# Row 0's experts as timed tasks among the scans of layer 0, and seven PSUM banks as one stock in layer 1

## What is computed

```python
def _L0_ffn_ref(x, scores, expert_weights, top_experts, w1, w2):   # w1 (256, 2048), w2 (2048, 256)
    order = jnp.argsort(flat_experts, stable=True)
    token_idx = order // TOP_K
    h = jax.nn.gelu(x_flat[token_idx] @ w1, approximate=True)
    y = h @ w2
    out = jnp.zeros((T, H)).at[token_idx].add(w_sorted[:, None] * y)
...
def _mamba_block(x, ...):
    xm, res = jnp.split(x @ in_proj_w.T, 2, axis=-1)
    xm = silu(conv(xm) + conv_b)                       # causal, 4 taps, per channel
    dt, Bm, Cm = jnp.split(xm @ x_proj_w.T, ...)
    delta = softplus(dt @ dt_proj_w.T + dt_proj_b)
    # h[t] = exp(delta[t] A) h[t-1] + delta[t] B[t] u[t];  y[t] = sum over 16 states of C[t] h[t]
    y = (scan(...) + u * D) * silu(res)
    return y @ out_proj_w.T
...
x = x + _L0_attn_ref(layernorm(x), ...) + _L0_ffn_ref(layernorm(x), ...)
x = x + _L1_attn_ref(layernorm(x), ...) + _L1_ffn_ref(layernorm(x), ...)
```

## Time and profile before

| | |
|---|---|
| median of 3 runs | 4269.71 us (4264.41 to 4275.40) |
| the profiled execution | 4272.54 us, span 4270.8 us |
| busy: PE, DVE, ACT, POOL | 3918.5, 3170.8, 2571.6, 2199.5 us |
| granted TensorE clock, mean | 0.955 of full speed |
| first scan; last gate of layer 0 | 187.73 us; 2022.57 us |

### The profile page before, as it was taken

The page is one execution under the profiler, slowest core; times in us unless marked ns, Lnnn a source line. Parts: engine busy times, 40 slices in busy tenths (PEclk is TensorE's granted clock), DMA queues, the critical chain, the costliest instruction groups (busy, mean ns, idle before and its releaser), DMA issues.

```text
span 4270.8 us, 60828 instructions
## 1 busy us (share of the span) xinstructions
PE 3918.5 (92%) x19232; PEld 2262.9 (53%) x19232; DVE 3170.8 (74%) x6060; ACT 2571.6 (60%) x3951; POOL 2199.5 (51%) x1724
## 2 busy tenths in 40 slices
PE   7988899999999899997889999999999999999997
PEld 4555555656565555565545545455455444544444
DVE  0299999999999999989474856748567585765753
ACT  3387778787888778775244454545554545545444
POOL 0299999999999899998211313213131131321311
PEclk9989999999999999998989999999999989999898
DMA  2254445545555555544311221212212122121210
GB/s 107 71 163 153 162 154 161 163 161 163 165 164 166 150 164 164 166 144 158 107 41 53 75 62 39 76 53 74 63 46 69 53 73 64 39 76 53 63 41 19
DMA packets 250177, 442.02 MB, mean 103 GB/s; under 512 B 25780, under 2 KB 80388, under 8 KB 248964
## 3 DMA queue, kind: packets, MB, share of 16 engines
q1 hardware_dynamic: 249860, 438.14, 33.1%
HBM read 366.39 MB, written 69.21 MB: 102 GB/s over the span
## 4 chain that ended last, share of the span: by engine, by line
PE 48%; DVE 8%; issue 4%; ACT 4%; POOL 2%; DMA 1%; SPq 0%; DVEq 0%; POOLq 0%; ACTq 0%
PE ps L1345 7%; PE ps L1453 6%; PE ps L1446 5%; PE ps L1307 5%; PE ps L1326 5%; PE ps L1376 3%; PE ps L1382 2%; DVE ps L1843 2%; PE ps L1209 2%; PE ps L1353 1%; PE ps L1429 1%; PE ps L1387 1%; DVE ps L1821 1%; PE ps L1258 1%; PE ps L1416 1%
## 5 line engine op out<-in xcount | busy, mean ns | idle before, releaser
L2066 POOL TENSOR_TENSOR drive<-du,b_wide 128x1024 f32<-128x1024 f32 x512 | 1201.1, 2361 | 173.1 <-DVE held L1821 96.9
L1470 ACT ACTIVATE exps<-ps 128x1024 f32<-128x1024 f32 (+3 forms) x768 | 620.4, 809 | 591.8 <-PE ps L1326 565.9
L2101 POOL TENSOR_SCALAR_AFFINE_SELECT exps<-exps 128x256 f32<-128x256 f32 x512 | 213.2, 419 | 1374.8 <-ACT exps L1470 1373.1
L1470 ACT ACTIVATE ps<-delta,neg_a 128x512 f32<-128x512 f32 x1024 | 681.0, 685 | 147.3 <-DVE heavy L1799 127.3
L1843 DVE CUSTOM_DVE_ANT_0 ps<-ps,later 128x128 f32<-128x128 f32 (+3 forms) x1024 | 484.4, 512 | 208.9 <-PE ps L1307 202.2
L1258 PE MATMUL ps<-p_all,heavy 128*128 128x128 f32 x3072 | 452.2, 283 | 89.4 <-DVE heavy L1799 78.7
L1258 PEld LDWEIGHTS ps<-p_all,heavy 128*128 128x128 f32 x3072 | 368.9, 145 | 257.3 <-DVE heavy L1799 139.8
L1799 DVE TENSOR_TENSOR heavy<-c_wide,ps 128x512 f32<-128x512 f32 x704 | 468.5, 670 | 1.0
L1821 DVE TENSOR_TENSOR_SCAN ps<-ps,carry,drive 128x512 f32<-128x512 f32 x352 | 441.2, 1272 | 16.7 <-ACT ps L1470 16.7
L1821 DVE TENSOR_TENSOR_SCAN ps<-ps,drive 128x512 f32<-128x512 f32 x352 | 420.6, 1214 | 26.2 <-ACT ps L1470 22.9
L1846 DVE TENSOR_REDUCE smax<-ps 128x2 f32<-128x1024 f32 x256 | 312.6, 1221 | 136.1 <-PE ps L1307 131.2
(11 more groups left out here) (193 smaller groups left out, 6475.3 us busy)
## 6 DMA issues: line engine op xcount, KB each, us to landing
b_wide<-bc_dram SPq DMA_DIRECT2D x512, 256.0 KB, 3.4
c_wide<-bc_dram SPq DMA_DIRECT2D x512, 256.0 KB, 3.6
stacks<-parts SPq DMA_DIRECT2D x192, 256.0 KB, 2.4
qs<-stacks SPq DMA_DIRECT2D x128, 192.0 KB
ks<-stacks SPq DMA_DIRECT2D x128, 192.0 KB, 4.2
x_row<-in_x SPq DMA_DIRECT2D x15, 1024.0 KB, 8.0
resid<-mix SPq DMA_DIRECT2D x9, 1024.0 KB, 5.3
x_row<-resid SPq DMA_DIRECT2D x9, 1024.0 KB, 6.5
```

What stands on the lines that cost most here:

```text
L1470: return nc.scalar.activation(out_, in_, func, **kw)
L2066: G.tensor_tensor(drive[:, g % DRIVE_SLOTS, :, :], du[:, e, :, :], wide(b_wide[:, g % B_SLOTS, :], MD), ALU.mult).then_inc(driven, 1)
```

## The change

Experts: `moe_pre0`, the loop above, `mlp_down`, `moe1`, `moe2` and `moe_h` are gone. The expert MLP is now four passes v (two halves of the hidden channels r, two halves of the row c), each of 8 `mh` units (up, copied by ACT into `h0`), one `gelu_t` of ACT over all of `h0`, and 4 `mo` units (down), which DVE adds to `mix` one by one. They are tasks of layer 0's list with ticks 32 steps a pass from tick 0 on, in the banks 6 and 7. Their weights go, a quarter of the experts' total at a time, through `w_up0` and `w_down0`, the buffers of the MLP of layer 0: SP loads the second halves (`expert_up`, `expert_down`), then the MLP's own weights (`up`, `down`), and stores row 0 (`first`) as tasks of the list. `h` of j = 0 comes after the last `mo`. The prelude keeps `xt` of the first half, `xm`, `cv`, `xd` and `dl` of j = 0; `res` of j = 0, the second half's `norm` and `xt` join the list. The row statistics of row 0 are taken in two halves, and x and the weights are loaded in two parts each.

Banks in layer 1: the pair [0, 1] becomes a third place for wide units, and a dense unit may take any of seven banks: bank 3 if it is free, else one whose neighbour is taken, else any.

```diff
 LENGTH0 = {..., "o": 4.0, "mu": 0.4, "var": 0.4, "mh": 1.74, "mo": 3.5}
+MOE_FROM, MOE_STEPS = 0, 32
...
+def moe_part(v):
+    return v // NC, v % NC
...
 def prelude_units():
-    out = [("xt", 0, c, k) for c in range(NC) for k in range(KD)]
-    for i in range(NC * ME):
-        out += moe_pre0(i) + [("moe", i // ME, i % ME)]
-    return out
+    return ([("xt", 0, 0, k) for k in range(KD)] + [("xm", 0, m) for m in range(MI)] + [("cv", 0, m) for m in range(MI)]
+            + [("xd", 0)] + [("dl", 0, m) for m in range(MI)])
...
+    for t in range(TC, NT):
+        add("a", ("norm", 0, t), 0.42 if t > TC else 3.2, t - TC - 2)
+    for c, k in [(1, k) for k in range(KD)]:
+        add("p", ("xt", 0, c, k), LENGTH0["xt"], 2 + k, ("a", "norm", 0, NT - 1))
+        add("a", ("xt", 0, c, k), EMPTY0["xt"], 2 + k, ("p", "xt", 0, c, k))
+    for t in range(TC):
+        add("p", ("res", 0, t), LENGTH0["res"], 26 + 2 * t)
+        add("a", ("res", 0, t), EMPTY0["res"], 26 + 2 * t, ("p", "res", 0, t))
+    add("a", ("silu_g", 0), 4.5, 36, ("a", "res", 0, TC - 1))
+    for v in range(MOE_PASSES):
+        r, c = moe_part(v)
+        at = MOE_FROM + MOE_STEPS * v
+        for m in range(MF):
+            add("p", ("mh", v, m), LENGTH0["mh"], at + MOE_STEPS * m / 16, ("a", "xt", 0, c, KD - 1),
+                ("p", "mo", v - 1, TC - 1) if v else None, only(r and c == 0, ("s", "expert_up")))
+            add("a", ("mh", v, m), EMPTY0["mh"], at + MOE_STEPS * m / 16, ("p", "mh", v, m))
+        add("a", ("gelu_t", v), 6.2, at + MOE_STEPS / 2, ("a", "mh", v, MF - 1))
+        for t in range(TC):
+            place = at + MOE_STEPS / 2 + MOE_STEPS * t / 8
+            add("p", ("mo", v, t), LENGTH0["mo"], place, ("a", "gelu_t", v), only(r and c == 0, ("s", "expert_down")))
+            add("v", ("mo", v, t), EMPTY0["mo"], place, ("p", "mo", v, t))
...
-WIDE_BANKS = ([4, 5], [6, 7])
-DENSE_BANKS = ([0], [1], [3])
+WIDE_BANKS = ([4, 5], [6, 7], [0, 1])
+DENSE_BANKS = ([3], [0], [1], [4], [5], [6], [7])
+PARTNER = {0: 1, 1: 0, 4: 5, 5: 4, 6: 7, 7: 6}
...
         if name in needs:
-            held[unit] = min(pools[pool_of(unit)], key=lambda pool: pool[0])
-            held[unit][0] = float("inf")
-            banks[unit] = held[unit][1]
+            fit = [choice for choice in choices[pool_of(unit)] if from_when(choice) <= start]
+            banks[unit] = min(fit, key=lambda one: (len(one[1]) == 1 and one[1][0] in PARTNER and
+                                                    1 + (bank_free[PARTNER[one[1][0]]] <= start), from_when(one)))[1]
+            for bank in banks[unit]:
+                bank_free[bank] = float("inf")
...
-            sp.dma_start(x_row0[:, :, :], x_in[0].rearrange("(t p) d -> p t d", p=P)).then_inc(x_fetched, 16)
-            sp.dma_start(moe1[:, :, :], moe1_in).then_inc(moe_in, 16)
-            sp.dma_start(w_l0[:, :], w_in[:, 0:L0_COLS]).then_inc(weights_in, 16)
-            sp.dma_start(moe2[:, :, :], moe2_in).then_inc(moe_in, 16)
+            for half, signal in ((slice(0, TC), x_first), (slice(TC, NT), x_fetched)):
+                sp.dma_start(x_row0[:, half, :], x_in[0].rearrange("(t p) d -> p t d", p=P)[:, half, :]).then_inc(signal, 16)
+                if half.start == 0:
+                    sp.dma_start(w_l0[:, 0:W_AT["in"][1]], w_in[:, 0:W_AT["in"][1]]).then_inc(weights_in, 16)
+            sp.dma_start(w_l0[:, W_AT["in"][1]:], w_in[:, W_AT["in"][1]:L0_COLS]).then_inc(weights_more_in, 16)
+            load_experts(0, True)
+            load_experts(0, False)
             sp.dma_start(mix[:, :, :], x_in[0].rearrange("(t p) d -> p t d", p=P)).then_inc(x0_in, 16)
...
+                elif kind == "expert_up":
+                    full(sp, L0_PLAN, ("mh", NC - 1, MF - 1))
+                    load_experts(1, True)
...
+                elif kind == "mh":
+                    r, c = moe_part(j)
+                    m = unit[2]
+                    drained(pe, L0_PLAN, ("xt", 0, c, KD - 1), "a")
+                    pe.wait_ge(expert_up_in, 16 * (r + 1))
+                    for k in range(KD):
+                        last = mm(bank, w_up0[:, k, m * P:(m + 1) * P], xT0[:, k, c * HALF:(c + 1) * HALF],
+                                  start=(k == 0), stop=(k == KD - 1))
+                elif kind == "mo":
+                    t = unit[2]
+                    pe.wait_ge(expert_gelu, j + 1)
+                    pe.wait_ge(expert_down_in, 16 * (moe_part(j)[0] + 1))
+                    for m in range(MF):
+                        last = mm(bank[:, 0:D], h0[:, m, t * P:(t + 1) * P], w_down0[:, m, :], start=(m == 0),
+                                  stop=(m == MF - 1))
...
+                elif kind == "gelu_t":
+                    drained(act, L0_PLAN, ("mh", j, MF - 1), "a")
+                    f(h0[:, :, :], h0[:, :, :], ACT.Gelu_apprx_tanh).then_inc(expert_gelu, 1)
...
+                elif kind == "mo":
+                    (r, c), tt = moe_part(task[1]), task[2]
+                    t = TC * c + tt
+                    bank = full(dve, L0_PLAN, task)
+                    V.scalar_tensor_tensor(mix[:, t, :], bank[:, 0:D], ew_sum[:, t:t + 1], mix[:, t, :], ALU.mult,
+                                           ALU.add).then_inc(drained_v, 1)
```

235 lines of the change are left out of this document (112 added, 123 removed).

## The result

The changed kernel takes 4168.23 us (median of 4 runs, 4166.9 to 4176.46) against 4272.56 us for the kernel before on the same chip (4 runs, 4264.41 to 4283.51). The ratio is 0.9758, with a 95% interval of 0.9732 to 0.9784: faster by 2.4%. The profiled execution has a span of 4173.8 us where the one of before had 4270.8, that is 97.0 us less. The forecast was 4180. By the medians the gain is 104.3 us: the profiled execution of the changed kernel happens to be the slowest of its four.

What follows compares the result with a forecast made beforehand. PE was busy 92% of the span; in the scans DVE set about 55 us per pair, PE where its share was large. Terms -121 + 60 + 5 - 38 = -94 from 4272.5 gave 4178.5, stated as 4180 us, range 4115 to 4245.

Steps and rivals of the forecast that it cites:

- the signs: Profile if right: first scan 65 to 72, pair 3's gate 283 us later, last gate near 1967, layer 1 some 2209 us.
- signs of being wrong: Drive waits for b_wide after experts' loads; PE waits for gelu; layer 1 single-unit bank waits or clock below 0.95.
- Term 1: Start: with the experts moved out, the first scan comes at 67 instead of 187.7 us: -121 us (-116 to -123).
- Term 2: Scans: expert work lengthens pairs 0 to 3 by 55 us, pairs 4 to 7 by 1, ACT's gelu 4: +60 (+45 to +85).
- PE sets it: Scan pairs: where PE's share is large, PE sets the time; pairs 0 to 3 take 275 x 1.03 = 283 us.
- here PE is late anyway, so I put 1 us each: Pairs 0 to 3: DVE idles if decays run dry during ACT's four gelu passes, priced at +4 us.
- Term 3: SP's queue: four 1 MB loads and row 0's store among b_wide and c_wide loads: +5 us (0 to +30).
- Term 4: Layer 1: seven banks as one stock remove 40% of 92 us of waits, times 1.1: -38 us (-95 to +30).
- (a): Layer 1: the banks give nothing, 4214 us, or lose 30 on single banks, 4245 us; chance 0.19.
- (b): Both parts at their better end, term 2 at 45 and term 4 at -85: some 4110 us; chance 0.13.
- (c): Scans: PE stays at 91%, the first scan's lead is spent, banks alone decide: 4232 to 4270 us; chance 0.04.
- (d): Layer 1: some 740 single units each wait 0.25 us longer for their bank: slower, 4307 us; chance 0.05.

Runs made afterwards that it cites:

- e5: Changed kernel with the loops of each expert unit (mh, mo) cut to their first matmul call, same instruction order: 4163.49 us, ratio 0.974.
- e12: Changed kernel with expert units cut to their first matmul call and the list planned anew for the shorter units: 4163.47 us, ratio 0.9734.
- e7: On top of e3, row 0's second half normalised early, two transposed blocks and two mh units moved between cv and xd: 4135.66 us, ratio 0.9679.
- e3: Changed kernel with PARTNER emptied, so single units take whichever of seven banks has been free longest: 4144.85 us, ratio 0.9679.
- e8: Changed kernel with an expert pass every 48 scan steps instead of 32, spread over pairs 0 to 5: 4193.78 us, ratio 0.982.
- e10: Changed kernel with expert units cut to their first matmul call and each gelu pass replaced by a one-column copy: 4154.15 us, ratio 0.97.
- e1: Changed kernel with layer 1's old banks, so the experts' part alone: 4219.86 us, ratio 0.986.
- e4: Changed kernel with single units limited to banks 3, 0 and 1, scores keeping three pairs: 4181.29 us, ratio 0.9765.
- e6: Changed kernel with the second loads of the experts' weights cut from 1 MB to 4 KB each: 4167.89 us, ratio 0.9752.
- e2: Kernel before with only the planner's stock of seven banks, experts still ahead of the scans: 4224.3 us, ratio 0.9868.

## Why the prediction was right, and where a step was not

**Sum.** -94 forecast, -97.0 in the two profiles; four terms within 7 us each. One of them doesn't come out of its own working: 40% of 92 us, times 1.1, is 40.5 and not 38. Of the signs, first scan, gate of pair 3, PE's share and clock are as written; layer 1 took 2202.2 us for 2209; the last gate ended at 1971.6 for "near 1967", in four other executions with the same layer 0 at 1961.1 to 1966.3. Of the signs of being wrong, PE waited once for ACT's copy of an experts' tile (4.2 us), and layer 1's clock is 0.94, as in the kernel before over the whole layer.

**Term 1, the start: right in size and in its steps.** -120.1 instead of -121. One place was off: xd took 6.24 us where 3.44 and "perhaps a slow clock again" stood; its copy was out at 52.6, not 50, and dl, softplus, du and the first drive product followed some 2.6 us late. The margin between 65 and 67 took up 2 of these. The landing of b_wide did not matter. A table load again began right behind the copy before it (41.66 + 0.69 = 42.35, load at 42.37) and silu right behind the load (43.66), so the extra drain that the Trainium skill's page "ScalarE: Activation LUTs", section "What ACT_TABLE_LOAD costs", gives per switch does not show here either.

**Term 2, the experts in the scans: right in size, wrong in cause.** +60 forecast, +60.8 measured; pairs 0 to 3 in 284.8 us for 283, at PE 95% and clock 0.98, as written. The failed step is "PE sets it", PE work times 1.03. Taking 76 us of PE's work out gave 8.4 us of the 56.2 that the stretch had grown by (e5); with a newly planned list it gave 18.1, of which part came back later (e12); and moving two mh units and two transposes into an idle place gave nothing in these pairs (e7 against e3). The row that I should have weighed is the one I wrote off with "here PE is late anyway, so I put 1 us each": DVE waits 35 us for decays, 28 more than before, and its own work in these pairs is 10.3 us more (228.1 against 217.8). In the new list ACT copies 32 h tiles out, runs four gelu passes and 25 table loads (20 in those pairs of before), and the decays stand in one queue with all of it: 31.6 of the 35 us end behind a load back to the exponential, as the trace shows above. That several engines, each in a fixed order, hold the stretch in turn, so that no single removal gives back its own time, is my reading of this. That PE's 95% and the count times 1.03 gave the number was luck; e8 breaks it: the same PE work in 529.3 us.

What stays open: with PE's expert work and the gelu passes both gone (e10), pairs 0 to 3 still take 268.0 us, 39.4 more than before. DVE's busy time accounts for 9.3 of it (227.2 - 217.8), its waits for decays for 17.4 (24.4 in e10 against 7.0), and smaller waits of several kinds for the rest. Where the late decays stand is in the trace; that ACT's fixed order, with the switches of function and the copies between them, makes the waits was not tried, neither by moving the passes nor by a list planned anew without both.

The +7.3 from pair 8 on, for which I had no term, is that one execution's and not the change's: in the same stretch e1, e3, e4 and e6 take 1387.8, 1385.8, 1385.6 and 1387.7 us with the same order as the changed kernel, and the kernel before 1386.1.

**Term 3, SP's loads: 5 forecast, nothing found,** inside its bounds. Two of the four transfers cost nothing (e6). The queue's own waits stay in that run, but drive products wait for b_wide only twice in pairs 0 to 7, for 3.1 us at 87.6, before any of the loads, and for 1.9 us at 354.5, behind the store and the last load; in the kernel before it is 3.4 + 1.1 us.

**Term 4, the banks: right in kind, a little small.** -38 forecast; -45.0 between the two profiles, -44.6 from before to e2, -56.6 from e1 to the changed kernel, each give or take some 12. The mechanism is the one described: short returns of pairs fall (236 to 142 with the pv units counted in, as in the prediction; 517 to 217 in the table, which counts only units that own a bank), and the waits of the score units fall by 43%, for 40% forecast. Three things were missing. Other waits grew by 19.5 us, so that PE's idle time fell by 26.7 and not by the 46.2 of the score units. PE's busy time fell as well (2088.5 to 2070.2), which makes up the 45.0; that both errors nearly cancel is luck. And the rule of choice costs: without its two leanings layer 1 is 21.9 us shorter. I had named bank 3 as a risk (107 of 128 f1 units; 84 in e3) and priced it against the old rotation instead of against the other choices of the same stock; whether bank 3 or the other leaning costs it stays open.

**Rivals.** (a) "The banks give nothing" is refuted by e2, with it the Trainium skill's case in "TensorE: Matmul & The Clock Gate", section "HAM oscillation — how this bites in real kernels", as a guide for this kernel: more banks helped where waits were for readers. (b) did not come: even e3 reached only 4145. (c) the lead was not lost: 59.3 of the 120.1 us stayed up to pair 7. (d) did not come: over layer 1 all waits outside the sm and st units grew by 19.5 us together, not by 185.
